# Two-layer vision block on one core: the end of the second stage reordered, two recurrence steps in three passes of split operands

## The reference

```
xn = _ln(x, norm1_scale, norm1_bias)
u = xn @ Wu + bu
g = sigmoid(xn @ Wg + bg)
h = 0
for _ in range(8):
    h = g * (h @ A) + (1.0 - g) * u
x = x + h
xn2 = _ln(x, norm2_scale, norm2_bias)
m = gelu(xn2 @ mlp_w1 + mlp_b1) @ mlp_w2 + mlp_b2
return x + m
```

## Time and profile before

| what | us |
|---|---|
| median of 3 runs (lowest, highest) | 231.0 (230.25, 231.27) |
| the profiled execution | 230.03 |
| its span, first to last instruction | 228.2 |
| TensorE busy | 219.4 (96%) |
| VectorE busy | 183.1 (80%) |
| GpSimd busy | 148.9 (65%) |
| ScalarE busy | 137.5 (60%) |

### The profile page before, as it was taken

One profiled execution on the slowest core, in us unless ns is written; L12 is line 12 of the kernel. 1 busy time (PEld: TensorE's weight loads), 2 busy tenths in 40 slices (PEclk: granted clock), 3 DMA queues, 4 the chain that ended last, 5 costly groups with the idle time before them and its releaser, 6 DMA issues.

```text
span 228.2 us, 4139 instructions
## 1 busy us (share of the span) xinstructions
PE 219.4 (96%) x1332; PEld 182.2 (80%) x1332; DVE 183.1 (80%) x462; ACT 137.5 (60%) x309; POOL 148.9 (65%) x179
## 2 busy tenths in 40 slices
PE   8999796999999999999999999999999999999985
PEld 5696665889898979787987688788888888788784
DVE  7799999999999998995168986978796958586641
ACT  5766784878787766756744395546264563515352
POOL 6564786778889877949677374666658472927230
PEclk9999999999999999999999999999999999999999
DMA  4861000000000000000000012030404032021012
GB/s 110 212 195 40 1 0 0 4 0 0 3 1 0 3 1 0 3 0 0 0 3 0 1 70 72 34 105 34 138 4 146 27 102 73 34 73 34 0 40 66
DMA packets 11973, 9.31 MB, mean 41 GB/s; under 512 B 1232, under 2 KB 11696, under 8 KB 11952
## 3 DMA queue, kind: packets, MB, share of 16 engines
q1 hardware_dynamic: 11664, 8.97, 13.1%
q10 hardware_dynamic: 288, 0.09, 0.2%
HBM read 5.31 MB, written 3.74 MB: 40 GB/s over the span
## 4 chain that ended last, share of the span: by engine, by line
PE 78%; DVE 11%; DMA 5%; SPq 2%; issue 1%; ACT 1%; POOL 0%; DVEq 0%
PE bank L1407 12%; PE pA L1407 9%; PE pM L1700 9%; PE pM L1358 8%; PE bank L1532 7%; DMA x_all<-in_x 5%; DVE cA L1073 4%; DVE cB L1073 2%; PE bank L1575 2%; PE bank L1474 2%; PE bank L1580 2%; PE pA L1445 2%; PE bank L1457 2%; PE pM L1350 2%; PE pM L1346 2%; PE pM L1347 2%
## 5 line engine op out<-in xcount | busy, mean ns | idle before, releaser
L426 POOL TENSOR_TENSOR rs<-var,power 128x4 f32<-128x4 f32 x32 | 32.5, 1015 | 22.5 <-DVE var L964 18.8
L1073 DVE SCALAR_TENSOR_TENSOR cA<-pA,cols,cA 128x528 f32<-128x528 f32 x54 | 40.7, 754 | 0.2
L1700 PEld LDWEIGHTS pM<-w,hid 128*128 128x128 f32 x192 | 29.7, 191 | 5.6 <-ACT hid L916 1.2
L1358 PEld LDWEIGHTS pM<-w,hid 128*128 128x128 f32 x192 | 28.4, 191 | 5.7 <-issue 1.0
L1153 DVE SCALAR_TENSOR_TENSOR q<-th,bank 96x256 f32<-96x256 f32 x48 | 19.2, 412 | 13.3 <-PE bank L1407 13.3
L1700 PE MATMUL pM<-w,hid 128*128 128x96 f32 x192 | 28.8, 267 | 0.8 <-ACT hid L916 0.8
L1358 PE MATMUL pM<-w,hid 128*128 128x96 f32 x192 | 28.9, 266 | 0.0
L1407 PE MATMUL pA<-q,a_half 96*96 96x256 f32 x96 | 27.0, 380 | 0.2 <-DVE q L1153 0.2
L1073 DVE SCALAR_TENSOR_TENSOR cB<-bank,cols,cB 128x256 f32<-128x256 f32 x56 | 26.4, 472 | 0.0
L559 POOL TENSOR_TENSOR xl<-xt,xh 96x512 fp32r<-96x512 f32 x11 | 14.1, 1283 | 17.1 <-ACT xh L894 17.1
L1532 PE MATMUL bank<-local,mix 128*128 128x384 f32 x64 | 24.8, 497 | 0.1
(11 more groups left out here) (249 smaller groups left out, 608.5 us busy)
## 6 DMA issues: line engine op xcount, KB each, us to landing
moved<-blocks SPq DMA_DIRECT2D x11, 192.0 KB, 1.9
xt<-moved SPq DMA_DIRECT2D x33, 64.0 KB, 2.0
x_all<-in_x SPq DMA_DIRECT2D x8, 192.0 KB, 2.9
out<-y SPq DMA_DIRECT2D x7, 192.0 KB, 2.1
w<-in_w SPq DMA_DIRECT2D x1, 480.0 KB, 5.8
w<-in_w SPq DMA_DIRECT2D x1, 336.0 KB, 3.5
mix<-in_mix SPq DMA_DIRECT2D x1, 256.0 KB, 3.7
out<-y SPq DMA_DIRECT2D x2, 96.0 KB, 1.7
```

The lines of the kernel that those rows point to most:

```text
L426: pool.tensor_tensor(rs[:, :], var[:, :], power[:, :], ALU.pow).then_inc(step, 1)
L1073: dve.scalar_tensor_tensor(out=acc, in0=src, scalar=col(f"k{'AB'[grp]}{k}"), in1=acc, op0=ALU.mult, op1=ALU.add).then_inc(s["conv_step"], 1)
L1358: last = pe.matmul(psum[:, k * D:(k + 1) * D], hid[:, j * TILE + k * P:j * TILE + (k + 1) * P], wc0("w2", j * D, (j + 1) * D), start=(j == ...
L1700: last = pe.matmul(dst, hid1[:, j * TILE + k * P:j * TILE + (k + 1) * P], wc1("m2", j * D, (j + 1) * D), start=j == 0 and (k == 0 if whole ...
```

## The change

In tiles 1 to 7 steps 3 and 5 of the recurrence (`SPLIT_STEPS`) no longer multiply float32 q by float32 `a_half`. ScalarE copies q to `q_high` (float32r), VectorE forms `q_low` = q - q_high, and TensorE makes three passes: a_high q_high, a_low q_high, a_high q_low. `a_high` and `a_low` are made once, in `turn`. The input products 1 and 2 both stand ahead of step 3 now, and none behind it. On VectorE `turn_blocks3` moves from behind step 2 to behind step 4, `ln3_stats` from ahead of step 5 to behind it; SP stores and loads the blocks of the second norm first. At the end the transposes of h go ahead of the input products of tile 6, the output products of tile 6 go to bank 3 (`V_BESIDE`) and no longer wait for y, the last tile's output products are done for its first half first, VectorE scales two of the last tile's four row groups instead of one, and GpSimd's last addition waits for them.

ScalarE, `body1` and the last tile's rows:

```
-                        scale_rows(xn4, x4, rs4, s["xn4_ready"], range(3))
+                        scale_rows(xn4, x4, rs4, s["xn4_ready"], range(2))
...
                 gelu(0)
+                split_q_high(c, 0)
                 gelu(1)
                 if not is_last(m):
                     normalize4(m)
                 gelu(2)
+                split_q_high(c, 1)
                 evac_gu(f)
```

VectorE:

```
-                for k in (3,):
+                for k in (2, 3):
...
                     ln4_last(m)
-                    store_sum(g)
+                    store_sum(g, V_BESIDE)
...
                 step(c, 2)
                 if peeled(f, 2):
                     ln3_low(f)
-                turn_blocks3(i + 2)
+                split_q_low(c, 0)
...
                 step(c, 4)
+                split_q_low(c, 1)
+                turn_blocks3(i + 2)
+                step(c, 5)
                 ln3_stats(i + 3)
-                step(c, 5)
                 if tile_known(f):
                     first_h(f)
                 step(c, 6)
```

GpSimd, for the last tile, and TensorE:

```
+                    if is_last(m):
+                        pool.wait_ge(s["xn4_ready"], 4 * m + 4)
                     add_row(x4b[m % 2][:, :], x4[:, :], rows[:, 2 * D:3 * D], s["x4b_ready"])
...
-M1_LAST = (2, 3, 1)
+M1_LAST = (2, 4, 1)
...
-                                else:
+                                elif is_last(u):
+                                    pe.wait_ge(s["y_ready"], u - 1)
+                                elif not ln4_beside(u):
                                     pe.wait_ge(s["y_ready"], u)
...
-                    m2(g, *range(12))
+                    m2(g, 0, 1, 4, 5, 8, 9, 2, 3, 6, 7, 10, 11)
...
                 if is_last(m):
+                    h_transposes(m)
                     m1(0)
-                    h_transposes(m)
                     m1(1)
                     m1(2)
...
                 m1(1)
-                rec_step(c, 3)
                 m1(2)
+                for h in range(2):
+                    split_step(c, 0, h)
...
                 for h in range(2):
-                    rec_step(c, 5, [h])
+                    split_step(c, 1, h)
                     m2(g, 4 + h)
```

More of the change, by code:

```diff
@@ L71 @@
 VIA_DRAM = 3
-M1_LAST = (2, 3, 1)
+M1_LAST = (2, 4, 1)
+V_BESIDE = 3
+SPLIT_STEPS = (3, 5)
 REC_BANK = (4, 2, 5, 3)
@@ L194, in build @@
         q_one, q_three = sb("q_one", TILE), sb("q_three", TILE)
+        a_high, a_low = sb("a_high", D, F32R), sb("a_low", D, F32R)
+        q_high, q_low = sb("q_high", TILE, F32R), sb("q_low", TILE, F32R)
         h8 = sb("h8", TILE)
@@ L387, in _ @@
                 n, m, p = c + 2, c - 1, c - 3
+                if ln4_moved(m):
+                    store_blocks(blocks4, moved4, "blocks4_done", "moved4_stored", "xt4_loaded", m)
                 if VIA_DRAM <= n < TILES:
@@ L390, in _ @@
                 if ln4_moved(m):
-                    store_blocks(blocks4, moved4, "blocks4_done", "moved4_stored", "xt4_loaded", m)
+                    load_moved(xt4, moved4, "moved4_stored", "xt4_loaded", "x4_lo", m, m)
                 if VIA_DRAM <= n < TILES:
                     load_moved(xt3, moved3, "moved3_stored", "xt3_loaded", "x3_lo", n if n > VIA_DRAM else 0, n - VIA_DRAM)
-                if ln4_moved(m):
-                    load_moved(xt4, moved4, "moved4_stored", "xt4_loaded", "x4_lo", m, m)
                 if tile_known(p):
@@ L582, in turn @@
                 ln3_std(3)
+                pool.wait_ge(s["a_high_ready"], 1)
+                pool.tensor_tensor(a_low[0:D, :], a_half[0:D, :], a_high[0:D, :].bitcast(F32), ALU.subtract)\
+                    .then_inc(s["a_low_ready"], 1)
             def body1(i):
@@ L902, in turn @@
                 normalize3(2)
+                act.activation(a_high[0:D, :], a_half[0:D, :], ACT.Copy).then_inc(s["a_high_ready"], 1)
             def body1(i):
@@ L1155, in step @@
                            .then_inc(s["q_ready"], 1)
+            def split_q_low(c, n):
+                if tile_known(c):
+                    k = SPLIT_STEPS[n]
+                    for h in range(2):
+                        dve.wait_ge(s["q_high_ready"], 4 * (c - 1) + 2 * n + h + 1)
+                        dve.wait_ge(s["q_ready"], QS * c + 2 * k + h - 1)
+                        dve.tensor_tensor(q_low[0:D, half(h)], moved(c, k)[0:D, half(h)],
+                                          q_high[0:D, half(h)].bitcast(F32), ALU.subtract).then_inc(s["q_low_ready"], 1)
             def first_h(c):
@@ L1183, in turn, with store_sum @@
                 last_h(0)
-            def store_sum(p):
+            def store_sum(p, at=V_BANK):
                 dve.wait_ge(s["x4b_ready"], p + 1)
@@ L1188, in store_sum @@
                 dve.wait_ge(s["m2_done"], p + 1)
-                dve.tensor_tensor(y[:, :], bank[V_BANK][:, 0:384], x4b[p % 2][:, :], ALU.add).then_inc(s["y_ready"], 1)
+                dve.tensor_tensor(y[:, :], bank[at][:, 0:384], x4b[p % 2][:, :], ALU.add).then_inc(s["y_ready"], 1)
             def body1(i):
@@ L1409, in rec_step @@
                           .then_inc(s["step_done"], 1)
+            def split_step(c, n, h):
+                if tile_known(c):
+                    if c == 1:
+                        pe.wait_ge(s["a_high_ready"], 1)
+                        pe.wait_ge(s["a_low_ready"], 1)
+                    dst, first = step_bank(SPLIT_STEPS[n], h), SPLIT_STEPS[n] not in (1, 3)
+                    pe.wait_ge(s["q_high_ready"], 4 * (c - 1) + 2 * n + h + 1)
[3 more added lines that the diff above has]
+                    pe.matmul(dst, a_high[0:D, :], q_low[0:D, half(h)], start=False, stop=True, skip_group_check=True)\
+                      .then_inc(s["step_done"], 1)
             passes = ((wi_h, xh1), (wi_l, xh1), (wi_h, xl1))
@@ L1694, in m2 @@
                                     pe.wait_ge(s["x3_ready"], TILES)
-                                else:
+                                elif is_last(u):
+                                    pe.wait_ge(s["y_ready"], u - 1)
+                                elif not ln4_beside(u):
                                     pe.wait_ge(s["y_ready"], u)
                             whole = not is_last(u)
-                            dst = bank[V_BANK][:, k * D:(k + 1) * D] if whole else \
+                            dst = bank[V_BESIDE if ln4_beside(u) else V_BANK][:, k * D:(k + 1) * D] if whole else \
                                 bank[(V_BANK, 7)[k // 2]][:, (k % 2) * D:(k % 2 + 1) * D]
```

9 lines of the change are left out of this document (7 added, 2 removed).

## The result

| what | before | after |
|---|---|---|
| median of the runs (lowest to highest), us | 230.62 (230.21 to 231.27), 4 runs | 248.12 (247.6 to 248.6), 4 runs |
| the profiled execution, us | 230.03 | 247.87 |
| its span, us | 228.2 | 246.1 |
| mean granted TensorE clock | 1.00 | 0.979 |

The changed kernel is slower: ratio 1.0765, 95% interval 1.0739 to 1.0791, +17.5 us. The sign was forecast; the forecast of 236.9 us and its upper end of 241.0 are far too low.

A forecast was written before the change was run, and what follows sets the result against it. TensorE's own matmuls were taken to bound every turn, without waits. The terms, -2.1 + 2.7 + 2.2 + 4.1 - 1.0 = +5.9 us on the profiled 230.0, gave 236.9 us for the median of 231.0; range 229.8 to 241.0.

The forecast's parts named there:

- passes, both steps: Steps 3 and 5 of tiles 1 to 7: three passes save 0.076 us in each of 28 halves, -2.1 us.
- fill behind step 3: Between steps 3 and 4: with no input product there, TensorE stalls 0.39 us in each of 7 tiles, +2.7 us.
- ln3_stats: VectorE at turn's end: statistics ahead of first_h delay the next step 0 in tiles 1 to 4, +2.2 us.
- blocks3, SP's order: SP's changed order of storing and loading blocks: xt3 is used 1.9 us after its estimated landing, so no cost.
- port: VectorE's q_low and GpSimd hold each other up at SBUF; step 6 starts late in tiles 1 to 6, +4.1 us.
- end: After the last step 6: earlier h transposes gain 0.9 us and the reordered last products 0.1, -1.0 us.
- rival A: GpSimd gets the port between q_low's halves at step 3, delaying step 4 by 1.0 us seven times: 240.7 us, chance 0.17.
- The moved product itself costs nothing more: The third input product, moved ahead of step 3, adds no time and covers the splitting there.
- Nothing takes it up later: The 0.74 us stall before step 0 in tiles 1 to 4 is not recovered, as that tile's next step is TensorE-bound.
- B: The port costs nothing because VectorE and GpSimd miss each other: +2.9, 233.9 us, chance 0.19.
- C: VectorE keeps up and both stalls, behind step 3 and step 5, are covered: -3.1, 227.9 us, chance 0.14.
- D: Passes gain nothing, the end is gained, stalls are half as long: about 231.5 us, no change, chance 0.12.

The follow-up runs named there:

- GpSimd held back: The changed kernel with one wait added, so GpSimd's low half of x and additions to hs follow both q_low of step 3: 236.73 us, +5.8 over the kernel before.
- order alone: The changed kernel with steps 3 and 5 in full precision again, all splitting out and the new order of the queues kept: 238.04 us, +7.1 over the kernel before.
- the cover of step 3: The kernel before with the reordered end, and only the third input product moved on TensorE from behind step 3 to ahead of it: 233.14 us.
- ln3_stats behind step 5: The kernel before with the reordered end, and only ln3_stats moved from ahead of step 5 to behind it: 234.53 us.
- blocks3 and the loads: The kernel with the reordered end and late ln3_stats, plus blocks3's transpose behind step 4 and SP in the changed kernel's order: 234.67 us against 234.53.
- spare matmuls: The changed kernel with three unused matmuls ahead of split step 3 in tiles 2 and 6: median 243.82 us, 243.47 without one execution of 250.32 us.
- the end alone: The kernel before with only the diff's reordered end, everything ahead of it unchanged: 230.26 us, ratio 0.9969, -0.7 us.
- the faster version: The kernel before with the reordered end, step 5 alone in three passes, and GpSimd's x4b held until q_low: 228.87 us against 230.96; without that wait 230.78.

## Why the prediction was right or wrong

| term | forecast | measured | from |
|---|---|---|---|
| passes, both steps | -2.1 | -1.3, with the 0.5 of shorter cover and other waits in it | GpSimd held back less order alone |
| fill behind step 3 | +2.7 (+2.2 for whole steps) | +3.2 | the cover of step 3 |
| ln3_stats | +2.2 (alone 3.0) | +4.6 | ln3_stats behind step 5 |
| blocks3, SP's order | 0 | +0.1 | blocks3 and the loads |
| port | +4.1 | +6.7 | the 11.7 of GpSimd held back less the clock |
| granted clock | no term | +5.0 | spare matmuls, without the execution of 250.32 us |
| end | -1.0 | -0.7 | the end alone |

The measured column adds up to 17.6, where 17.5 was to be explained. Most of that agreement is built in, since each kernel is taken less the next; what could have failed is that the parts of the order, 3.2 + 4.6 + 0.1, make up the 7.8 of the order alone. Medians of four to ten runs leave each entry some tenths of doubt. The division of the 11.7 between port and clock rests on the spare matmuls alone, and the 6.7 of the port are net of what holding GpSimd back costs.

**Passes, end, blocks3: right.** 12.16-us turns with step 5 split and transposes 5.28 us behind step 6 show the first two directly. The sum of rival A is off by a tenth in its own terms: -2.1 + 2.7 + 7.0 + 3.0 - 1.0 is +9.6, not +9.7.

**Fill: right in its working**, 0.31 against 0.31 in a plain tile. The step that failed beside it is "The moved product itself costs nothing more": in tile 1 it waits 0.5 us for its own operand where it now stands, and it makes the work behind it late, so that h meets GpSimd once and tiles 2 and 4 are longer by more than the stall.

**ln3_stats: the step that failed is "Nothing takes it up later".** The stall itself, 0.67 us a tile, was forecast at 0.74. But the delay pushes h<-hs,q into GpSimd's xl<-xt,xh, and the h transposes stall as well. From h transposes to h transposes, turn 4 with the stall of step 0 alone is 0.64 us longer than with the new end, turn 5 with that of h alone 0.70, turns 2 and 3 with both 1.33 and 1.35. The port was looked for at the new operations only, not at the old ones that the change makes later.

**Port: the mechanism was right, and in the forecast it was put at the wrong step.** The forecast let both halves of q_low at step 3 pass and pushed xl<-xt,xh behind them, and put the 0.85 us at step 5. In the trace a GpSimd operation is served between the halves in tiles 3, 4, 5 (xl<-xt,xh) and 7 (hs<-hs,q_one), and both halves are held in tiles 1, 2 and 6; all nine waits for q_low are at step 3, and step 5 stalls nowhere. The row that said so was at hand, the statistic that got the port as soon as hs<-hs,q_three let go. The rule of the Trainium skill that the prediction cites ("SBUF — State Buffer", Who interferes with whom), that each holds the pair for its whole instruction, is borne out: 1.27 us becomes 1.45 and 0.42 becomes 1.49, as each waits for the end of the other's.

**Clock: missing.** The prediction read the granted clock of 1.00 and priced every stall at it. In tiles 2 and 6 three waits follow closely, 1.8 and 1.6 us idle in all, and the clock falls; in tiles 3, 4, 5 and 7, with 0.9 us, it does not. Stalls need not bring it down: with GpSimd held back, 4.9 us of waits left it at 1.00. The Trainium skill says in "TensorE: Matmul & The Clock Gate", Part 1, that the clock follows how busy the array has been of late. The trace agrees: 0.92 us of work in 2 us, and then 0.50. With it, A's 240.7 us would have carried a risk of some us more, and the range would have had to be open upward.

So the sign was right, by stalls of the kind that was forecast; what failed is the port's step and size, the statistics' effect on h, and the missing clock. Rivals B, C and D are excluded: q_low is not at 0.42 (B), the stalls are not covered (C), and they are not half as long (D).

## What to carry to other kernels

Where VectorE and GpSimd both read two tensors from SBUF, a new operation on the one is costed with the instruction that the other may slip in ahead of each of its halves; if the other has slack, a wait that orders the two is cheaper than letting them meet (11.7 us here, and 2 in the faster version). That holds for old operations too, once a change makes them late. A stall on a fully busy TensorE is priced with its restart, and where several fall together a fall of the clock may come on top. Make the chain longer only where cover stands ahead of it: the same splitting gained at step 5, behind the gate products (228.87 us), and lost when step 3 was split as well (233.72, with GpSimd held back in both).
